# Moving the end of each router and its softmax behind later matmul groups in an eight-pass transformer layer

## The reference

```
x = x + attention(layernorm(x))      # channel attention, 8 heads of 16 channels
x = x + ffn(layernorm(x))
ffn:  Q, K = x @ W_Q.T, x @ W_K.T;  invQ, invK = Q @ W_inv.T, K @ W_inv.T
      branch(Q_side, K_side):
        xV = Q_side @ V[k];  cum_yW = cumsum over tokens of K_side @ W[k]   # 8 experts, rank 64
        h = gelu(Q_side @ router_w1.T + b1);  weights = softmax(h @ router_w2.T + b2)
        out = (sum_k (xV * cum_yW * weights_k) @ U[k].T + weights @ b) / (token number)
      (branch(Q, K) + 0.5 * branch(invQ, invK)) @ W_O.T
```

## Time and profile before

| | us |
|---|---|
| median of 3 timed runs | 1539.8 (1538.19 to 1541.72) |
| the profiled execution | 1534.98 |
| its span on core 6, the slowest | 1533.5 (the cores: 1514.6 to 1533.5) |
| PE busy in the span | 1314.8 (86%) |
| DVE busy | 445.4 (29%) |
| ACT busy | 417.2 (27%) |

### The profile page before, as it was taken

How to read it: one execution, slowest core, us unless ns; L and a number is a source line. 1 busy time by engine, 2 the same in 40 slices (tenths; PEclk the granted TensorE clock), 3 DMA queues, 4 the chain that set the end, 5 groups by cost and what they waited for, 6 DMA issues and landing times.

```text
span 1533.5 us, 16860 instructions; the slowest of 8 cores (1514.6 to 1533.5 us)
## 1 busy us (share of the span) xinstructions
PE 1314.8 (86%) x5496; PEld 511.0 (33%) x5496; DVE 445.4 (29%) x756; ACT 417.2 (27%) x523; POOL 45.8 (3%) x90
## 2 busy tenths in 40 slices
PE   1496777439899889998998999899989999999897
PEld 0142222114334333433343334333433343334332
DVE  0002333341253125312431333143315321630151
ACT  2235443123231223132312231213222223213200
POOL 0010000000000000000000000000000000000000
PEclk9798887669999999999999999999999999999999
DMA  7747667752203620453045206410631162116101
GB/s 167 155 141 201 191 178 207 164 219 110 110 1 129 201 110 0 147 183 110 1 164 177 99 1 207 177 56 7 242 137 55 55 235 95 56 55 220 56 1 55
DMA packets 35970, 186.93 MB, mean 122 GB/s; under 512 B 2152, under 2 KB 2176, under 8 KB 27056
## 3 DMA queue, kind: packets, MB, share of 16 engines
q0 software_dynamic: 10928, 135.52, 27.9%
q1 hardware_dynamic: 24960, 50.33, 9.8%
HBM read 172.31 MB, written 31.46 MB: 133 GB/s over the span
## 4 chain that ended last, share of the span: by engine, by line
PE 68%; DMA 21%; DVE 4%; ACT 3%; issue 3%; DVEq 0%; ACTq 0%; POOLq 0%; SPq 0%
PE pb L344 64%; DMA outT<-ybuf 6%; DMA ybuf<-xT 6%; DMA xt<-xT 4%; PE pb L839 2%; DMA wsB<-WKT 1%; DMA wsA<-WQT 1%; ACT hsb L852 1%; DVE ybuf L760 1%; DMA wsA<-WOT 1%; PE pb L903 1%; PE pb L866 1%; DMA scr_WQT<-wsA 1%; ACT L852 1%; DMA wsB<-Ui 1%
## 5 line engine op out<-in xcount | busy, mean ns | idle before, releaser
L344 PE MATMUL pb<-Qfm,wsC 128*128 128x512 bf16 x512 | 127.5, 397 | 19.2 <-DVE ybuf L760 19.2
L852 ACT ACTIVATE hsb<-pb,r1bS 128x512 bf16<-128x512 f32 x128 | 87.3, 687 | 196.9 <-PE pb L344 193.3
L344 PE MATMUL pb<-Qfm,wsA 128*128 128x512 bf16 x512 | 126.7, 395 | 0.0
L344 PE MATMUL pb<-yb,wsA 128*128 128x512 bf16 x512 | 114.0, 384 | 7.9 <-DVE yb L815 7.9
L344 PE MATMUL pb<-ff,wsC 128*128 128x512 bf16 x512 | 113.6, 383 | 1.0 <-ACT ff L976 1.0
L344 PE MATMUL pb<-yb,wsB 128*128 128x512 bf16 x512 | 111.8, 379 | 0.0
L760 DVE TENSOR_TENSOR ybuf<-ybuf,pb 128x512 f32<-128x512 f32 x64 | 44.0, 687 | 216.5 <-DMA ybuf<-xT 179.7
L830 ACT CAST Qfm<-pb 128x512 bf16<-128x512 f32 x64 | 37.4, 585 | 198.4 <-PE pb L344 198.4
L809 DVE TENSOR_TENSOR lntmp<-ybuf,pb 128x4096 bf16<-128x4096 f32 x8 | 35.4, 4422 | 144.7 <-PE pb L344 144.7
L344 PEld LDWEIGHTS pb<-Qfm,wsC 128*128 128x128 bf16 x512 | 47.4, 101 | 86.6 <-issue 43.5
L344 PEld LDWEIGHTS pb<-yb,wsA 128*128 128x128 bf16 x512 | 50.6, 99 | 71.0 <-issue 12.2
(11 more groups left out here) (220 smaller groups left out, 1309.4 us busy)
## 6 DMA issues: line engine op xcount, KB each, us to landing
xt<-xT SPq DMA_DIRECT2D x8, 2048.0 KB, 13.9
ybuf<-xT SPq DMA_DIRECT2D x8, 2048.0 KB, 14.6
wsA<-scr_WQT POOLq DMA_DIRECT2D x8, 2048.0 KB, 8.0
wsB<-scr_WKT POOLq DMA_DIRECT2D x8, 2048.0 KB, 8.0
wsC<-scr_R1T POOLq DMA_DIRECT2D x8, 2048.0 KB, 9.7
wsA<-scr_R1TI POOLq DMA_DIRECT2D x8, 2048.0 KB, 10.1
wsB<-scr_UFUI POOLq DMA_DIRECT2D x8, 2048.0 KB, 8.3
wsC<-scr_WOT POOLq DMA_DIRECT2D x8, 2048.0 KB, 8.1
```

What stands on the lines that cost most here:

```text
L344: insts.append(eng.matmul(o, l, r, start=(i == 0), stop=(i == n - 1)))
L852: e.activation(hb, b["f32"][:, 0:SB], AF.Gelu, bias=r1bS[:, jc:jc + 1]),
```

## The change

Nothing is added to or taken from the work. `emit_h` no longer issues the end of a router (the eighth logit matmul, the copy on DVE, the release of its bank); it returns it as a function, and calls one handed in (`finish_prev`) after the gelu of its own first group. So the end of router F and its `emit_smx_pre` are issued within router I, after its first eight matmuls. The end of router I, its `emit_smx_pre` and its `emit_smx_mid` are issued in the hook of `emit_ywxv` for F, after xv of kc = 0 and ahead of `emit_smx_back` for F.

```diff
--- before.py
+++ after.py
@@ -830,7 +830,7 @@
                    e.copy(dst[:, oc * SB:(oc + 1) * SB], b["f32"][:, 0:SB]),
                    reads=[bq["res"]], writes=[res[dkey]], tag=f"B_{nm}ev{s}_{oc}")
 
-    def emit_h(s, bs, wname, lgsb, lgkey):
+    def emit_h(s, bs, wname, lgsb, lgkey, finish_prev=None):
         wt, wres = wuse(s, wname)
         blg = take_bank(pin=True)
 
@@ -851,13 +851,20 @@
             ae(lambda e, b=bh, hb=hb, jc=jc:
                e.activation(hb, b["f32"][:, 0:SB], AF.Gelu, bias=r1bS[:, jc:jc + 1]),
                reads=[bh["res"], res["r1bS"]], writes=[hbr], tag=f"B{bs}_hev{s}_{jc}")
+            if jc == 0 and finish_prev is not None:
+                finish_prev()
             if pend is not None:
                 lg_mm(*pend)
             pend = (jc, hb, hbr)
-        lg_mm(*pend)
-        ve(lambda e, b=blg, lgsb=lgsb: e.tensor_scalar_add(lgsb, b["f32"][0:8, 0:SB], bias2),
-           reads=[blg["res"], res["bias2"]], writes=[res[lgkey]], tag=f"B{bs}_lgev{s}")
-        unpin(blg)
+
+        def finish():
+            lg_mm(*pend)
+            ve(lambda e, b=blg, lgsb=lgsb:
+               e.tensor_scalar_add(lgsb, b["f32"][0:8, 0:SB], bias2),
+               reads=[blg["res"], res["bias2"]], writes=[res[lgkey]],
+               tag=f"B{bs}_lgev{s}")
+            unpin(blg)
+        return finish
 
     def emit_smx_pre(s, bs, lgsb, lgkey, wts, wtsk):
         btA = take_bank(pin=True)
@@ -1008,19 +1015,22 @@
         if s + 1 < NSB:
             emit_load(s + 1, extra=(fence1 if s + 1 == 1 else ()))
             emit_proj(s + 1)
-        emit_h(s, "F", "R1T", lgsbF, "lgsbF")
-        emit_smx_pre(s, "F", lgsbF, "lgsbF", wtsBF, "wtsBF")
+        finF = emit_h(s, "F", "R1T", lgsbF, "lgsbF")
         wstream(s, "UFUI")
         wstream(s, "WOT")
-        emit_h(s, "I", "R1TI", lgsbI, "lgsbI")
-        emit_smx_pre(s, "I", lgsbI, "lgsbI", wtsBI, "wtsBI")
+        finI = emit_h(s, "I", "R1TI", lgsbI, "lgsbI",
+                      finish_prev=lambda s=s, f=finF:
+                      (f(), emit_smx_pre(s, "F", lgsbF, "lgsbF",
+                                         wtsBF, "wtsBF")))
         emit_smx_mid(s, "F", wtsBF, "wtsBF")
         if s + 1 < NSB:
             wstream(s + 1, "WQT")
-        emit_smx_mid(s, "I", wtsBI, "wtsBI")
         emit_ywxv(s, "F", Vfb, "Vfb", Wfb, "Wfb", carryF, "carryF",
-                  hook=lambda s=s: emit_smx_back(s, "F", wfmF, "wfmF",
-                                                 wtsBF, "wtsBF"))
+                  hook=lambda s=s, f=finI:
+                  (f(),
+                   emit_smx_pre(s, "I", lgsbI, "lgsbI", wtsBI, "wtsBI"),
+                   emit_smx_mid(s, "I", wtsBI, "wtsBI"),
+                   emit_smx_back(s, "F", wfmF, "wfmF", wtsBF, "wtsBF")))
         emit_ywxv(s, "I", Vixb, "Vixb", Wiyb, "Wiyb", carryI, "carryI",
                   hook=lambda s=s: emit_smx_back(s, "I", wfmI, "wfmI",
                                                  wtsBI, "wtsBI"))
```

## The result

| | before | changed |
|---|---|---|
| median of 20 timed runs, us | 1539.73 | 1549.61 |
| ratio of the runs | | 1.0055 (95% interval 1.004 to 1.007) |
| profiled execution: span of the slowest core | 1533.5 | 1546.8 |
| mean granted clock, median core of each die | 0.940, 0.937 | 0.931, 0.931 |

A second comparison (e8) gave 1.0067 (1.0041 to 1.0094). By the ratio the change costs 8.5 us; the forecast was 5.1. The effect is small, but a ratio of 1 lies outside the interval. Some runs of both kernels, in which a whole die ran at a lower clock, are in the medians and left out of the ratios.

A forecast was written before the change was run, and what follows sets the result against it. The prediction took PE to bound the kernel, with 68% of the chain that ended last. Waits of -6.1 at F and +7.8 at I plus +3.4 of clock made +5.1 us, forecast 1544.9 us, range 1533 to 1553.

The forecast's parts named there:

- F, wait: Step from router F to router I: the gelu wait goes, saving 0.76 us a pass, 6.1 us in eight.
- I, wait: Step from router I to the first emit_ywxv: DVE's queue delays the I copy, 0.98 us a pass, +7.8 us.
- Clock at F: Step from router F to router I: the shorter poor stretch halves the clock's cost, from 10.6 to 5.4 us.
- Clock at I: Step from router I to the first emit_ywxv: one fall a pass certain, a second likely, 16.5 us against 7.9.
- Nothing behind it on DVE or ACT costs PE: After the step from router I to emit_ywxv: DVE, some 0.4 us late, catches up, and PE loses nothing.
- the first, rival 1: Clock never falls at F and falls once a pass at I: -5.2 us, 1534.6 us, faster; chance 0.20.
- The second: I wait at its low end, clock falls only shift from F to I: -1.0 us, 1538.8 us; chance 0.22.
- The third: Two clock falls in every pass at I, waits at the high end: +16.2 us, 1556.0 us; chance 0.12.
- The fourth: DVE's queue doesn't hold the I copy, so both places save 0.76 us a pass: 1527.6 us; chance 0.02.

The follow-up runs named there:

- e8: The changed kernel itself, measured a second time against the kernel before, on another chip: ratio 1.0067.
- e7: The changed kernel with ten extra dense matmuls, their sum never read, behind the eighth logit matmul of I: ratio 0.9966 to the kernel before.
- e3: The changed kernel with the sums and scaling of F on DVE issued behind the copy of the I logits: ratio 0.9990 to the kernel before.
- second traces: Second profiles, on another chip, of the kernel before (one time, 1543.6 us) and of the unaltered changed kernel (ratio 1.0067).
- e9: The kernel before with only the F place of e6 (logit matmul and copy behind group 0 of router I, transposes behind group 1): ratio 0.9864.
- e6: The kernel of e4 with the weight transposes of F moved behind yw of kc = 1: ratio 0.9707 to the kernel before, median 1500.4 us.
- e4: The changed kernel with logit matmul and copy one group ahead of the transposes, and I's copy ahead of F's sums: ratio 0.9747 to the kernel before.

## Why the prediction was right, and where its sizes were off

It said slower, 5.1 us, by less saved at F than lost at I, and the time lay in its range, which was wide (1533 to 1553, so that no change and a small gain lay in it too). By its steps (a "poor stretch" is time in which PE has only waits, transposes and a logit matmul):

- **F, wait: -6.1 forecast.** Right. The stretch at full clock went from 20.0 to 19.2 us, 4.54 us where 4.58 was forecast, and the wait for the copy stayed at 1.0 us.
- **I, wait: +7.8 forecast.** The mechanism was right and the size a little off. DVE's chain came out as worked out, the first transpose at +6.84 in e7 and +6.83 in the changed kernel; e3 shows that the sums ahead of the copy hold it. But yw1 stood at +9.10 where the clock didn't fall, not +9.34: the four logit transposes take 1.02 us up to the next one also when transposes follow, and I had taken 1.25. That makes 0.74 in this pass, 5.9 us for eight like it; the windows of e7 give 5.6 (195.6 less 190).
- **Clock at F: -5.2 forecast.** This term was mis-sized. It took half, 5.4, of a cost of 10.6 that came from two cores. Measured over all cores the cost was 8.9 us before (168.7 less 8 x 19.98) and 8.4 after (162.2 less 8 x 19.22); the second traces have 10.3 and 7.2. So the change took 0.5 us of it away, or 3.1 by the second traces, and not 5.2. Falls came in 41 and 47 of 64 stretches before, in 42 and 36 after. The step that failed is that the shorter stretch would halve them. A poor stretch of 2.4 us trips the clock nearly as often as one of 3.4; only without a wait (e9) did the falls stop.
- **Clock at I: 16.5 forecast, from 7.9.** Right. A fall in each of 64 stretches; the fillers of e7 gave 14.2 us of its cost back with nine falls left, and 211.6 less eight stretches at full clock (8 x 24.45, the mean of the rows of e7) makes 16.0. Before it was 7.6 (197.6 less 190).
- **Nothing behind it on DVE or ACT costs PE.** Right: the only wait for DVE's products that PE shows went from 2.2 to 2.5 us in the whole kernel (`P2I`), and e6, with the work closer still, runs at 22.08 us in every I stretch.

So -6.5 and +14.0 stand where the forecast had -11.3 and +16.4. F came out 4.8 us worse and I 2.4 better, and it is luck that the two errors partly cancel. The waits alone sum to about nothing (-6.1 and +5.6 to 5.9), so nearly all of the loss is the clock behind the I place. The rivals: the first (F never falls) is refuted by 42 falls. The second (waits and clock cancel) fails since falls at I became certain. The third (two falls in each pass) isn't there: the I rows of core 4 are one fall in six and a longer one in two, and over all cores the longer one is in 28 of 64, in e8 in 34. The forecast's 16.5, between one and two a pass, had this right. The fourth is refuted by the wait of 2.58 us at I, and e3 shows that DVE's queue makes it.

The rule of the Trainium skill that rival 1 leaned on ("TensorE: Matmul & The Clock Gate", Part 1, HAM oscillation: long waits between bursts re-throttle the clock) agrees with the traces in part. At I the clock fell in all 64 stretches with a wait of 2.6 us, and in 9 with work in that gap (e7). But in e3 it fell in all 64 with no wait above 1.0 us there, and at F one wait of 1.0 us with four small transposes was enough in 42 and 36 of 64. So the length of the longest wait isn't what decides in this kernel.

## What to carry to other kernels

Moving the end of a chain behind other work hides only those links for which a whole group of work then stands between producer and consumer; here the gelu got one and the copy on DVE got none, so split the chain at each hand-over and put a group between (e6). Before moving a small step on a busy engine, write down what stands ahead of it in that engine's new order: here sums and a scan that nobody needed yet stood ahead of a 0.74 us copy. And price a stall of PE with the clock behind it: at the I place 5.6 to 5.9 us more of waiting came with some 8 us more of lower clock, and ten useless matmuls in the wait gained 1.0%.

## What the hardware did that I had not expected

- Adding ten dense matmuls a pass (2.33 us in the timeline) to an idle stretch made the kernel 15.6 us faster (e7 against e8 on one chip), with falls in 9 instead of 64 stretches.
- In the three traces with a shortened stall at F, the clock fell more often behind another one 20 us later, in 53, 44 and 43 of 64 passes against 30 and 27, in code that wasn't touched.
- The clock fell in all 64 I stretches of e3 although PE waited there for 0.99 and 0.81 us at most, with small transposes between.
- With four plus four small transposes and no wait (e4), 2.3 us, the clock fell in 21 of 64 stretches; with the same transposes in blocks of 1.0 and 1.25 us (e6) in none.
